# Value projections of layer 0 made inside its attention block instead of ahead of it

## The reference, cut to what matters

```python
q = split_heads(query @ Wq.T + bq)      # query = layernorm(x), 4 x 512 x 256
k = split_heads(key @ Wk.T + bk)        # key = value = ctx, 4 x 512 x 256
v = split_heads(value @ Wv.T + bv)      # 16 heads of 16
scores = jnp.einsum('bhqd,bhkd->bhqk', q, k) / sqrt(16) + relative_bias
attn = softmax(where(key_padding_mask, scores, -inf))
out = jnp.einsum('bhqk,bhkd->bhqd', attn, v) @ Wo.T + bo
```

## Time and profile before

| | before |
|---|---|
| median of 3 runs | 944.98 us (939.49 to 4893.35) |
| the profiled execution's own time | 940.07 us |
| its span, first to last instruction | 938.3 us |
| mean granted TensorE clock | 0.975 |
| PE, DVE, ACT, POOL busy | 895.9, 563.9, 452.2, 459.9 us |

### The profile page before, as it was taken

The page is one execution under the profiler, slowest core; times in us unless marked ns, Lnnn a source line. Parts: engine busy times, 40 slices in busy tenths (PEclk is TensorE's granted clock), DMA queues, the critical chain, the costliest instruction groups (busy, mean ns, idle before and its releaser), DMA issues. The chain is left out here.

```text
span 938.3 us, 20996 instructions
## 1 busy us (share of the span) xinstructions
PE 895.9 (95%) x7733; PEld 555.0 (59%) x7734; DVE 563.9 (60%) x1659; ACT 452.2 (48%) x645; POOL 459.9 (49%) x648
## 2 busy tenths in 40 slices
PE   7889999999989999999999999997999899999998
PEld 2466555555567455556555555574555677777765
DVE  4558989899828334367999999757522222222226
ACT  2426767788745233346777777833111122323221
POOL 2017878888847600017888888741264022222224
PEclk9987999999999999986999999999999999999999
DMA  9853535453143331344242424033822021212216
GB/s 327 307 207 115 181 113 169 146 165 108 32 144 104 131 111 64 121 146 112 69 123 71 123 69 126 22 94 147 252 86 92 11 68 58 68 57 68 62 60 238
DMA packets 70372, 111.82 MB, mean 119 GB/s; under 512 B 17574, under 2 KB 41578, under 8 KB 68106
## 3 DMA queue, kind: packets, MB, share of 16 engines
q1 hardware_dynamic: 62458, 91.26, 31.6%
q0 software_dynamic: 3408, 9.38, 2.8%
q10 hardware_dynamic: 4416, 9.96, 2.8%
HBM read 76.99 MB, written 33.58 MB: 118 GB/s over the span
## 5 line engine op out<-in xcount | busy, mean ns | idle before, releaser
L745 ACT ACTIVATE pT<-ps 128x1024 f32<-128x1024 f32 x224 | 219.9, 1027 | 86.5 <-PE ps L615 86.4
L795 POOL TENSOR_SCALAR s<-s,nmax 128x512 f32<-128x512 f32 x218 | 148.5, 693 | 171.8 <-DVE nmax L686 168.1
L795 POOL TENSOR_SCALAR xT<-xT,nmax 128x512 f32<-128x512 f32 x224 | 153.2, 694 | 55.5 <-DVE nmax L686 55.4
L686 DVE CUSTOM_DVE_ANT_0 xT<-ps,bias 128x512 f32<-128x512 f32 x240 | 156.3, 688 | 23.8 <-PE ps L601 14.5
L686 DVE CUSTOM_DVE_ANT_0 s<-ps,bias 128x512 f32<-128x512 f32 x224 | 145.8, 688 | 11.8 <-PE ps L601 5.8
L601 PE MATMUL ps<-ks,qs 49*128 49x512 f32 (+1 forms) x512 | 140.8, 511 | 5.9 <-DVE nmax L686 3.1
L633 PE MATMUL ps<-pT,vq 128*32 128x512 f32 x1024 | 137.2, 612 | 2.9
L601 PEld LDWEIGHTS ps<-ks,qs 49*128 49x128 f32 (+1 forms) x512 | 57.6, 199 | 115.4 <-DVE nmax L686 88.2
L1683 POOL DMA_INDIRECT slots_out<-y,id x39 | 37.7, 967 | 140.2 <-DVE y L2019 136.8
L1767 PE MATMUL ps<-gu,xgT 128*128 x312 | 98.9, 460 | 0.7 <-ACT xgT L1851 0.7
L2013 DVE TENSOR_TENSOR hs<-gs,ps 128x352 f32<-128x352 f32 x39 | 20.3, 520 | 105.4 <-ACT gs L1856 105.4
(11 more groups left out here) (202 smaller groups left out, 1207.3 us busy)
## 6 DMA issues: line engine op xcount, KB each, us to landing
bias<-in_bias SPq DMA_DIRECT2D x13, 1024.0 KB, 7.6
qs<-qk_scratch SPq DMA_DIRECT2D x180, 64.0 KB, 2.4
ks<-qk_scratch SPq DMA_DIRECT2D x62, 128.0 KB, 2.9
gu<-in_gate_up SPq DMA_DIRECT2D x8, 704.0 KB, 8.8
slots_in<-zeros SPq DMA_DIRECT2D x4, 1280.0 KB, 6.3
xg<-slots_in SPq DMA_DIRECT2D x39, 130.0 KB, 2.1
qk_scratch<-parts ACTq DMA_DIRECT2D x8, 512.0 KB, 5.5
qk_scratch<-parts SPq DMA_DIRECT2D x8, 512.0 KB, 5.0
```

The costliest lines, as they stand in the source:

```text
L686: nc.vector.tensor_tensor_reduce(at.s[n % 4][:, k, :], sb.ps[:, ring_bank(tile_place[u]), :], at.bias[bias % BIAS_SLOTS][:, k, :], -1.0, 3 ...
L745: nc.scalar.activation(at.pT[:, slot(m // HG, m % HG), 2 * half:2 * half + 2, :], sb.ps[:, 2 + 2 * half:4 + 2 * half, :], ACT.Exp).then_in ...
L795: nc.gpsimd.tensor_scalar(s, s, -1.0, at.nmax[:, n % 4, k:k + 1], ALU.mult, ALU.add).then_inc(pool_less_max, 1)
```

## The change

The value projections leave `projection_phase` and go into `attention_phase`, for layer 0 alone (`at.first_late_v` is 0 there, and past the end in layer 1, where nothing is added). The eight pairs stay the same matmuls and the same DVE additions.

- Four pairs (i = 0 to 3) stand among the first eight score tiles, one behind each two tiles, in PSUM banks 6, 5, 4 and 3. The first turn waits until all four have been kept.
- Four pairs (i = 4 to 7) stand in the first four steps, half a pair ahead of the turn and half at the end of the step, all in bank 6, so each waits until the one before it has been kept.
- DVE keeps a pair behind two tiles of the first eight, and at the end of each of the first four steps.
- The first `values` wait for the last kept pair, and so do ACT's exponentials from step 4 on and SP's load of `bias_more`, since `pT` and `bias_more` now lie over weights and context that are still read. POOL's `keep_values` waits for the pairs of its batch.
- `v`, `bv` and `cT` are allocated behind `parts`, so that the attention's `s` lies over `qk` and the first two homes of `parts`. DVE waits for the stores of groups 1 and 4 (`at.stored_first`) ahead of its first tile.
- ACT's high stores of key groups 2 and 3 are issued at the start of the attention block and no longer between two `head` operations. Group 2 joins the early stores, and the late stores are waited for at step 2.

```diff
@@ projection_phase
-    at.loaded_ahead, at.joint_load = 2, True
-    at.stored_early = [(stored[g], 32) for g in KEY_EARLY + QUERY_EARLY]
+    at.loaded_ahead, at.joint_load, at.first_late_v = 2, True, 0
+    at.stored_first = [(stored[g], 32) for g in (KEY_EARLY[1], QUERY_EARLY[0])]
+    at.stored_early = [(stored[g], 32) for g in KEY_EARLY + QUERY_EARLY + KEY_LATE[:1]]
+    def store_late_heads(act):
+        for g in KEY_LATE:
+            store_head(act, g)
@@ projection_phase, PE and DVE
-            for v in range(NV):
-                project_v(v)
-            for v in range(NV):
-                keep_v(v)
@@ projection_phase, ACT
-            store_head(5)
-            for g in KEY_LATE:
-                store_head(g)
+            store_head(act, 5)
@@ attention_phase
+    late_v = range(at.first_late_v, TT // 2)
+    NV = len(late_v)
+    among_scores = max(NV - HG, 0)
+    def v_bank(i):
+        return 6 - i if i < among_scores else 6
@@ SP
                     if per_head_bias and first and b == 2:
+                        sp.wait_ge(v_copied, NV)
                         next_bias(hg, 0)
@@ PE
+            def project_v(i, halves):
+                if i == 0 and 0 in halves:
+                    pe.wait_ge(ld.v, 32)
+                if i > among_scores and 0 in halves:
+                    pe.wait_ge(v_copied, i)
+                for half in halves:
+                    t = 2 * late_v[i] + half
+                    for c in range(DC):
+                        last = nc.tensor.matmul(sb.ps[:, v_bank(i), half * D:(half + 1) * D],
+                                                w.cT[:, c, t * P:(t + 1) * P], w.v[:, c, :],
+                                                start=(c == 0), stop=(c == DC - 1))
+                if 1 in halves:
+                    last.then_inc(v_done, 1)
             def turn(hg, m):
+                if hg == 0 and m == 0 and among_scores:
+                    pe.wait_ge(v_copied, among_scores)
@@ PE, values
                 if kt == 0:
+                    if NV and hg == 0 and b == 0:
+                        pe.wait_ge(v_copied, NV)
@@ PE, the first tiles and the steps
             for u in range(0, AHEAD, 2):
                 scores(u)
+                if u // 2 < among_scores:
+                    project_v(u // 2, (0, 1))
...
+                    if NV and first and b == 0:
+                        project_v(among_scores + j, (0,))
                     turn(hg, m)
                     for i in range(early, early + late, 2) if u + early < len(order) else ():
                         scores(u + i)
+                    if NV and first and b == 0:
+                        project_v(among_scores + j, (1,))
@@ DVE
+            for stored in at.stored_first:
+                dve.wait_ge(*stored)
             for u in range(AHEAD):
                 add_bias(u)
+                if u % 2 and u // 2 < among_scores:
+                    keep_v(u // 2)
...
+                    if NV and first and b == 0:
+                        keep_v(among_scores + j)
@@ ACT
+            if at.store_late_heads is not None:
+                at.store_late_heads(act)
-                    for stored in at.stored_late if first and m == HG else ():
+                    for stored in at.stored_late if first and m == 2 else ():
                         act.wait_ge(*stored)
+                    if NV and first and m == HG:
+                        act.wait_ge(v_copied, NV)
```

More of the change, by code:

```diff
@@ L154, in projection_phase @@
     proj_done, head_done, low_done = sem(tag + "proj_done"), sem(tag + "head_done"), sem(tag + "low_done")
-    v_done, v_copied = sem(tag + "v_done"), sem(tag + "v_copied")
     NK = DC * B
     NT = 2 * NK
-    NV = TT // 2
     KEY_EARLY, KEY_LATE, QUERY_EARLY, QUERY_LATE = (0, 1), (2, 3), (4, 5), (6, 7)
@@ L190, in store_low, with store_head @@
         store(sp, g, 1)
+    def store_head(act, g):
+        act.wait_ge(head_done, 2 * g + 2)
+        store(act, g, 0)
     def store_late(sp):
@@ L195, in store_late @@
             store_low(sp, g)
-    at.store_late = store_late
+    def store_late_heads(act):
+        for g in KEY_LATE:
+            store_head(act, g)
+    at.store_late, at.store_late_heads = store_late, store_late_heads
     with nc.Block() as block:
@@ L244, in _ @@
         def _(pe):
[L245 to L258, removed]
             def turn(g):
@@ L319, in head @@
                                      bias=w.bqk[:, which, mo:mo + 1]).then_inc(head_done, 1)
-            def store_head(g):
-                act.wait_ge(head_done, 2 * g + 2)
-                store(act, g, 0)
             def root(i):
@@ L340, in _ @@
                 if n % 2:
-                    store_head(n // 2)
+                    store_head(act, n // 2)
             root(0)
@@ L350, in _ @@
             head(NK + 1)
-            store_head(4)
+            store_head(act, 4)
             keep_x(2)
@@ L376, in cut_parts @@
                                                part(n, 0), ALU.add, ALU.subtract).then_inc(low_done, 1)
[L378 to L382, removed]
             def statistics(b):
@@ L440, in _, with attention_phase @@
             nc.vector.tensor_scalar(w.bo[:, :], w.bo[:, :], sb.gates[:, 0:1], None, ALU.mult)
-def attention_phase(nc, sem, sb, at, dram, bias_dram, zeroed, tag):
+def attention_phase(nc, sem, sb, w, at, dram, ld, bias_dram, zeroed, tag):
     per_head_bias = bias_dram is not None
@@ L468, in attention_phase @@
     out_done = sem(tag + "out_done")
+    v_done, v_copied = sem(tag + "v_done"), sem(tag + "v_copied")
     GROUPS = H // HG
@@ L705, in normalise, with keep_v @@
                     ALU.mult).then_inc(out_done, 1)
+            def keep_v(i):
+                v = late_v[i]
+                dve.wait_ge(v_done, i + 1)
+                nc.vector.tensor_tensor(
+                    sb.v[:, 2 * v:2 * v + 2, :], sb.ps[:, v_bank(i), :].rearrange("p (a d) -> p a d", a=2),
+                    w.bv[:, :].unsqueeze(1).to_broadcast([P, 2, D]), ALU.add).then_inc(v_copied, 1)
+            for stored in at.stored_first:
+                dve.wait_ge(*stored)
             for u in range(AHEAD):
                 add_bias(u)
+                if u % 2 and u // 2 < among_scores:
+                    keep_v(u // 2)
             def body(hg, first, last):
@@ L799, in keep_values @@
                 pool.wait_ge(av_done, hg * B + b + 1)
+                made = sum(v < 2 * b + 2 for v in late_v)
+                if hg == 0 and made:
+                    pool.wait_ge(v_copied, made)
                 src = sb.v[:, b * QT:(b + 1) * QT, :].rearrange("p t (g f) -> p g t f", g=GROUPS)
@@ L2110, in projection_buffers, with context @@
         def projection_buffers(layer, made):
+            def context():
+                aw.v = made("v", [P, DC, D], F32)
+                aw.bv = made("bv", [P, D], F32)
+                aw.cT = made("cT", [P, DC, N], F32)
             aw.qk = made("qk", [P, 2, DC, D], F32)
-            aw.v = made("v", [P, DC, D], F32)
             aw.bqk = made("bqk", [P, 2, DC], F32)
-            aw.bv = made("bv", [P, D], F32)
-            aw.cT = made("cT", [P, DC, N], F32)
             if layer == 0:
@@ L2119, in projection_buffers @@
                 sb.parts = made("parts", [P, DC * B - 1, 2, 2, S], F32R)
+                context()
             else:
+                context()
                 sb.parts = made("parts", [P, PARTS, 2, S], F32R)
@@ L2149, in build @@
                 zeroed = sem("zeroed") if layer == 1 else None
-                attention_phase(nc, sem, sb, at, dr, a["bias"] if layer == 0 else None, zeroed, f"a{layer}_")
+                attention_phase(nc, sem, sb, aw, at, dr, ld, a["bias"] if layer == 0 else None, zeroed, f"a{layer}_")
             mem.close()
@@ L2188, in build @@
                     at.stored_early, at.stored_late = [(done, STORED) for done in stored], []
-                    at.store_late = None
+                    at.store_late, at.store_late_heads, at.stored_first, at.first_late_v = None, None, [], TT // 2
                     at.loaded_ahead, at.joint_load = 2, False
```

## The result

| | before | changed |
|---|---|---|
| median | 941.75 us (937.74 to 944.98, and one of 4893.35) | 945.14 us (942.34 to 947.09) |
| ratio to before, 95% interval | | 1.0033 [1.0017, 1.005] |
| profiled execution, span | 938.3 us | 944.3 us |
| first score tile of the attention block | 61.00 | 50.21 |
| first `values` | 80.72 | 86.84 |

By the ratio, the change makes the kernel 3.1 us slower. The forecast was 0.6 us faster.

A forecast was written before the change was run, and what follows sets the result against it. PE was taken to bound the kernel as a whole. Starting 11.7 us earlier, then 28.9 plus 2.75 for the clock, put first `values` at 80.95 against 80.72; 0.8 regained behind them gave 0.6 us faster, 939.5 from 940.07, range 933 to 947.5.

The forecast's parts named there:

- what is removed: Up to the attention block's first score tile: without the value projections it comes at 49.3 against 61.00, 11.7 us gained.
- the steps: Attention steps 2 and 3, turn to turn: 4.45 us each, 8.9 together, with the kept pair in the loop.
- The 2.6 ahead of the first `values`: After the fourth turn: another 2.6 us, since the first `values` wait for the last kept pair.
- the 0.8 behind them: From first `values` to the next tile: 0.99 us at full clock instead of 1.82 at low clock, 0.8 gained.
- what binds is the one bank 6: Steps 2 and 3: the single PSUM bank 6, with the kept pair in the loop, sets the 4.45 us.
- what the clock costs at the head: Start of the attention block: 5.5 us of dense work at half rate after the idle gap, costing 2.75 us.
- the sum of the first part: First score tile to first turn's end, full clock: tiles 1.6, projections 7.0, then wait and turn, 10.5 in all.
- Weight loads at the seams: First weight load of each value projection piece, behind other matmuls: taken as 0, most pieces beginning behind a wait.
- The bound of 2.3 for all pieces: Most that exposed first weight loads could cost over the 12 projection pieces: 12 x 0.19 = 2.3 us.
- behind it the steps should keep the full clock: After the half-rate stretch at the attention block's head: full clock kept, PE working four fifths of the time.
- the 6.9: From the end of the first turn to that of the second: 6.9 us at full clock.
- The rival of a second fall: Behind the first turn: clock falls again or returns late, three steps cost 8 us, 947.5 us; chance 0.13.

The follow-up runs named there:

- second trace: Profiled execution of the changed kernel measured once more, nothing altered, beside two other runs on one chip: 947.94 us, ratio 1.0073 to the kernel before.
- first trace: Profiled execution from the first measurement of the changed kernel, all value projections moved against the kernel before: 945.14 us, ratio 1.0033.
- two early pairs: Changed kernel with pairs 0 and 1 back in the projection block, in PE's gap before the barrier: 937.75 us, ratio 0.9968 to the kernel before.

## Why the prediction was wrong

**Right: what is removed.** The first tile was to come 3.6 us behind the query projections, and it came 3.5 behind them (46.70 to 50.21). The gain was 11.8 us, counted from the start of the query projections, where 11.7 were said, and what released the first tile was what had been named: the second gate operation on DVE ended at 49.75, 0.46 ahead of it, as before:

```profile
49.41 0.34 DVE L417 TENSOR_SCALAR bo<-bo,gates 128x256 f32<-128x256 f32 x1
```

In the second trace the query loads set the start (3.89 us, ended by the DMA), which had been named as a possible holder.

**Right in size: the steps.** 4.45 us a step were said, 4.56 and 4.58 measured, each with PE's wait for the kept pair (0.51, ended by DVE's L725). The 2.6 ahead of the first `values` were 2.5 (84.32 to 86.84), and the 0.8 behind them came back. But "what binds is the one bank 6" is too strong: with whole pairs ahead of the turn the wait for the bank was gone and the steps still took 4.64 us, because PE's own work then stood behind its wait for the ring. With that work inside the wait, a step of 3.81 us had no wait left.

**Wrong in size: what the clock costs at the head.** 2.75 us were taken, from bounds of 2 and 4. In the first trace it cost 4.55, since 15.72 us to the first turn became 11.17 when the gap was filled; in the second 1.6. The stretch at half rate was taken to be 5.5 us of dense work, and it was 9.7 in the first trace. The bounds came from the pace of the kernel's first projections, seen in one execution, and that pace can't be laid to the clock by the profile, which gives a granted clock of 1.00 there. The row of the kernel before for 12 to 14 us:

```profile
12.00:14.00 2.00, 2.00 (x4) 0.75 (x3) 1.02 (x4) 0.00 (x0) 0.00 (x0) 1.00 1.03 415
```

What halved the pace there no run shows, so the term rested on rows that don't show it.

**Wrong: the sum of the first part, 9.5 us to the first turn at full clock.** It measured 11.2. Two tiles and a pair take 2.58 us (59.90 to 62.48), where 2.15 were summed, and two terms share the difference of 1.7.

- Weight loads at the seams were taken as nothing. A pair takes 1.92 (60.56 to 62.48) and not 1.75, and half a pair 1.06 (75.59 to 76.65) and not 0.87: 0.19 more, the length of one weight load. That is 0.7 us up to the first turn. The bound of 2.3 for all pieces had been written down, and then the lower end was taken because most would begin behind a wait. PE waits in few of them, and where it does, the half pair costs the same (77.66 to 78.73).
- Two tiles were priced at 0.4 from the later steps, and take 0.66 here (59.90 to 60.56): 1.0 us for four of them. In `order` the first eight tiles are four of head 0 and four of head 1, which read the same 49 rows one behind the other; from then on the heads alternate, and with them the rows. In the kernel before, the third tile starts 0.53 us behind the first (61.00 to 61.53), so about half of the 0.26 is there without any projection, and three tiles in 0.93 against two in 0.51 had hinted at it. The other half comes with the projections around them. Whether the rows are the reason no run isolates.

The third tile of the kernel before, in a timeline of the window 61.7 to 62.2:

```profile
61.53 0.39 PE L601 MATMUL ps<-ks,qs 49*128 49x512 f32 x1
```

The Trainium skill's rule in "TensorE: Matmul & The Clock Gate", Part 3, that weight loads overlap only with matmuls of other row groups, would expose every load; the same part also names a background weight buffer into which a load is pulled ahead. The traces agree with the bare rule at the seams and not in a run of projections, where the loads of 0.19 are hidden in passes of 0.218, as they were before.

**Wrong: "behind it the steps should keep the full clock".** The clock fell a second time in both traces of the changed kernel, between the first two turns, which came 8.2 and 8.1 us apart instead of 6.9. In the second trace the half pair starts 5.0 us behind the end of the first turn (67.50), just as summed; only what follows is slow, the half pair with 2.0 and the turn with 1.7. At full clock the 6.9 would be 7.1, the 0.2 being the seam, so the low clock costs 1.1 us there in the first trace. In the second it reaches into the next step, which takes 6.3 us. The rival of a second fall had 0.13, was priced at 8 us for three steps, and was to be told by a clock of 0.50 between the third and the fourth turn. By that sign it didn't come: the clock is at 1.00 there in both traces. A shorter and earlier fall stood in no term. In the first trace PE was busy for 9.31 of the 10.20 us ahead of it.

Together: 31.65 were said from first tile to first `values`; 1.8 for the clock at the head, 1.7 for tiles and seams there, 1.3 between the first turns and 0.2 in the steps make 36.65, and 36.6 were measured. The forecast of 0.6 us was the difference of two numbers near 12. An error of 2 us in either was enough to turn its sign, and the larger misses all made the changed kernel slower. That the time still lies in the range is owed to its width, 14.5 us.

## What to carry to other kernels

Work moved off a stretch where the engine ran densely, into one with stalls, is paid back only by the waits that it fills. Ask what the piece stands behind in the engine's order: with a pair ahead of the turn a step took 4.64 us, with the same pair in the wait behind the turn 3.81. Moving it also opens a gap where it stood. Here that gap had a price of its own, and leaving two of the eight pairs in it took the kernel from 1.0033 to 0.9968. Take the price of an operation from a row where its neighbours and operands are laid out in the same way. And cut such work into few long pieces: here each seam cost a weight load.

## What the runs showed of the hardware that I had not expected

- The granted clock stayed at 0.50 for 9.7 us of PE work without a gap in one execution of the changed kernel (from 49.7, just ahead of the first tile). In another it fell 1.3 us behind the first tile and stayed down for 3.4. Both stretches came behind an idle gap of 3.5 to 3.9 us.
- A weight load of 0.19 us is exposed where value projections follow score tiles or a turn (1.06 for half a pair against 0.87 in the run of 64), though in that run each of the 64 loads is hidden.
- Two score tiles that read the same 49 rows one behind the other took 0.53 us to the next tile (61.00 to 61.53 before), and two of alternating heads 0.34 to 0.41 to the next operation.
- In the kernel before with its gap filled, where PE waits for DVE between single tiles, the clock fell at 64.8, after PE had been busy for 2.84 of 3.70 us. The gap ahead of that stretch was 0.64 us. With a gap of 1.51 and projections among the tiles it stayed at 1.00 for 14 us.
- The times of one kernel go with its mean granted clock: with two early pairs 932.05 us at 0.987 and 944.43 us at 0.975.
